# Who makes the low half of x's even blocks: VectorE from PSUM, or ScalarE and GpSimd through a copy

## The reference

```
mask = arange(L) < length[:, None]                 # one length per batch row
K    = 2 * Re(sum_n Cs[h,n] * exp(dtA[h,n] * l))   # one kernel of 1024 taps per head
y    = (causal convolution of x*mask with K + x*mask*D) * mask
logits = y @ route_w.T                             # 8 experts, the largest one is taken
wh   = one_hot(argmax) * max * (y @ A.T)           # 8 experts x rank 16 = 128 columns
out  = x + wh @ Bw
```

## Time and profile before

| what | value |
|---|---|
| median of 3 runs | 603.43 us (603.25 to 603.48) |
| profiled execution | 603.22 us |
| its span, first to last instruction | 601.4 us |
| mean granted TensorE clock | 0.996 of full speed |

### The profile page before, as it was taken

The page is one execution under the profiler, slowest core; times in us unless marked ns, Lnnn a source line. Parts: engine busy times, 40 slices in busy tenths (PEclk is TensorE's granted clock), DMA queues, the critical chain, the costliest instruction groups (busy, mean ns, idle before and its releaser), DMA issues.

```text
span 601.4 us, 13400 instructions
## 1 busy us (share of the span) xinstructions
PE 583.0 (97%) x3657; PEld 530.3 (88%) x3657; DVE 489.7 (81%) x1370; ACT 318.7 (53%) x1064; POOL 384.1 (64%) x519
## 2 busy tenths in 40 slices
PE   3899999999999999999999999999999999999996
PEld 2788999999999999999999899999999989999994
DVE  7978888888878888887887878788787887878875
ACT  4757566645554654654565464455546446445420
POOL 4687677576667657657666765866666685675430
PEclk9999999999999999999999999999999999999998
DMA  7133534533443443453454344345344434434521
GB/s 139 58 95 116 155 100 142 159 102 142 154 125 120 151 153 98 147 159 98 142 155 124 124 151 140 111 146 158 96 146 156 116 130 151 137 110 150 157 82 71
DMA packets 37583, 77.65 MB, mean 129 GB/s; under 512 B 12476, under 2 KB 20862, under 8 KB 37510
## 3 DMA queue, kind: packets, MB, share of 16 engines
q1 hardware_dynamic: 28358, 43.76, 28.8%
q10 hardware_dynamic: 9152, 33.03, 13.4%
HBM read 43.16 MB, written 33.62 MB: 128 GB/s over the span
## 4 chain that ended last, share of the span: by engine, by line
PE 90%; DVE 3%; POOL 2%; issue 1%; ACT 0%; ACTq 0%; POOLq 0%; DVEq 0%
PE psYo L1084 19%; PE psZ L1109 19%; PE psO L1084 15%; PE psYe L1084 12%; PE psS L1084 11%; PE psO L1134 4%; PE psXe L1098 4%; PE psXo L1098 4%; PE psZ L1168 1%; DVE psS L941 1%; POOL Xlo L505 0%; POOL Slo L512 0%; DVE Sf L945 0%; POOL Tlo L497 0%; POOL Glo L490 0%
## 5 line engine op out<-in xcount | busy, mean ns | idle before, releaser
L512 POOL TENSOR_TENSOR Slo<-Sf,Shi 128x384 fp32r<-128x384 f32 x64 | 65.4, 1022 | 165.3 <-ACT Shi L661 165.3
L941 DVE SCALAR_TENSOR_TENSOR psS<-Sf,tab,psS 64x128 f32<-64x128 f32 x256 | 91.9, 359 | 46.5 <-ACT Sf L656 39.6
L1109 PE MATMUL psZ<-Wt,Y 128*128 128x136 f32 x1024 | 129.2, 279 | 0.0
L1109 PEld LDWEIGHTS psZ<-Wt,Y 128*128 128x128 f32 x1024 | 123.3, 190 | 0.1
L656 ACT ACTIVATE Sf<-psS 128x128 f32<-128x128 f32 x64 | 17.8, 278 | 196.3 <-PE psS L1084 196.3
L980 DVE TENSOR_TENSOR ost<-psO,xt 128x512 f32<-128x512 f32 x128 | 87.8, 690 | 1.6 <-PE psO L1084 1.4
L505 POOL TENSOR_TENSOR Xlo<-xeven,Xhi 128x512 fp32r<-128x512 f32 x63 | 81.6, 1295 | 0.0
L473 POOL TENSOR_TENSOR both<-coarse,fine 128x512 f32<-128x512 f32 x64 | 68.3, 1067 | 1.3 <-ACT fine L601 1.2
L964 DVE TENSOR_TENSOR wlo<-psZ,whi 128x128 fp32r<-128x128 f32 x64 | 18.7, 292 | 40.4 <-ACT whi L666 40.4
L1084 PE MATMUL psO<-Bw_hi,whi 128*128 128x512 f32 x128 | 50.5, 395 | 0.7 <-ACT whi L666 0.7
L1084 PE MATMUL psO<-Bw_hi,wlo 128*128 128x512 f32 x128 | 50.8, 397 | 0.0
(11 more groups left out here) (200 smaller groups left out, 1526.7 us busy)
## 6 DMA issues: line engine op xcount, KB each, us to landing
xt<-in_x_dram SPq DMA_DIRECT2D x64, 512.0 KB, 4.9
out_dram<-ost ACTq DMA_DIRECT2D x63, 512.0 KB, 5.1
Traw<-kdram SPq DMA_DIRECT2D x64, 128.0 KB, 2.9
kdram<-krow SPq DMA_DIRECT2D x64, 1.0 KB
A_nat<-in_L_ffn_A_dram SPq DMA_DIRECT2D x1, 512.0 KB, 5.5
B_nat<-in_L_ffn_Bw_dram SPq DMA_DIRECT2D x8, 64.0 KB, 3.6
out_dram<-ost SPq DMA_DIRECT2D x2, 256.0 KB, 2.0
lens_i<-in_itok_B_dram SPq DMA_DIRECT2D x1, 64.0 KB, 4.9
```

The costliest lines, as they stand in the source:

```text
L512: pool.tensor_tensor(Slo[h.s2][:, :], Sf[h.s2][:, :], Shi[h.s2][:, :].bitcast(F32), ALU.subtract).then_inc(slo_done, 1)
L941: dve.scalar_tensor_tensor(psS[to, new], Sf[h.s2][fr, old], tab2[fr, BR, h.n:h.n + 1], psS[to, new], ALU.mult, ALU.add).then_inc(brought_d ...
L1109: last = pe.matmul(psZ[:, 0:NW], Y[:, j, c, :], Wt[:, 2 * c + j, :], start=(j == 0 and c == 0), stop=(j == 1 and c == NE - 1), skip_group_ ...
```

## The change

VectorE makes the low part of both halves of x, straight from PSUM, for every head. ScalarE's copy `x_even`, its buffer `xeven` and its semaphore, and GpSimd's subtraction `x_lo` are dropped. In VectorE's step the subtraction of the odd blocks moves from in front of the routing chain to behind `b_lo`, and the subtraction of the even blocks stands right before it there; both are then in front of `w_lo`. `turn_x` now waits for `xlo_even` of the head before instead of for the copy.

```diff
@@ buffers and semaphores
-        xeven = sb("xeven", [P, HALF])
-        xeven_done = sem("xeven_done")
@@ GpSimd
-            def x_lo(h):
-                need(pool, xeven_done, h.n)
-                need(pool, y_mm, (h.n - 1) * 2)
-                pool.tensor_tensor(Xlo[h.s2][:, 0, :], xeven[:, :], Xhi[h.s2][:, 0, :].bitcast(F32),
-                                   ALU.subtract).then_inc(xlo_even, 1)
...
-                if head(1).there:
-                    x_lo(head(1))
@@ ScalarE
-            def x_even(h):
-                need(act, xlo_even, h.n)
-                act.activation(xeven[:, :], psX[0][:, :], ACT.Copy).then_inc(xeven_done, 1)
...
                 if head(1).there:
-                    x_even(head(1))
                     t_hi(head(1))
@@ VectorE
             def x_lo_even(h):
                 need(dve, xhi_done, h.n * 2 + 1)
+                need(dve, y_mm, (h.n - 1) * 2)
                 dve.tensor_tensor(eo(Xlo[h.s2], 0), psX[0][:, :], eo(Xhi[h.s2], 0).bitcast(F32),
                                   ALU.subtract).then_inc(xlo_even, 1)
...
                     carry(head(0))
-                if head(1).there:
-                    x_lo(head(1))
                 if head(-1).there:
                     largest(head(-1))
...
                     turn_k(head(2))
                     b_lo(head(2))
+                if head(1).there:
+                    x_lo_even(head(1))
+                    x_lo(head(1))
                 if head(-1).there:
                     w_lo(head(-1))
@@ TensorE, turn_x
-                if is_head(h, 1) and j == 0:
-                    pe.wait_ge(xlo_even, 1)
-                else:
-                    need(pe, *((xlo_odd, h.n) if j else (xeven_done, h.n - 1)))
+                need(pe, xlo_odd if j else xlo_even, h.n)
```

More of the change, by code:

```diff
@@ L551, in _ @@
             t_lo(first[0])
-            x_lo(first[1])
             g_lo(first[1])
@@ L750, in _ @@
             s_hi(first[0])
-            x_even(first[1])
             g_hi(first[1])
@@ L1066, in _ @@
             clamp(parts[1])
+            x_lo_even(first[1])
+            x_lo(first[1])
             turn_k(first[2])
```

## The result

The changed kernel takes 619.25 us (median of 4 runs, 618.52 to 621.6) against 603.45 us for the kernel before (median of 4, 603.25 to 603.75): a ratio of 1.0269, 95% interval 1.0245 to 1.0293. The profiled execution's span is 617.9 us, 16.5 more than before. The forecast was 621.5 us for that execution, 621.7 for a median, within 612 to 631.

What follows compares the result with a forecast made beforehand. TensorE was taken to bound the steady loop. A 0.23 us wait plus 0.08 us weight load, 0.31 per step over 59 steps, added 18.3 us: 621.5 us profiled, 621.7 median, range 612 to 631.

Steps and rivals of the forecast that it cites:

- TensorE bounds the step, slack 0.15 us: Steady loop: TensorE waits for nobody, and `wlo` is ready 0.15 us before `up` would have to wait.
- Only 0.12 us of the moved subtraction come back: Before the routing chain: of the odd subtraction's 0.60 us, 0.12 return; the rest becomes VectorE's wait for `project`.
- E: The end of `project` in a step, from which later starts are counted in us.
- The rival by which the cover holds: Routing chain starts early enough that `wlo` is in time and nothing changes: 603.4 us, chance 0.08.
- The pair takes 1.20 us: Before `wlo`: the even and odd subtractions from PSUM together occupy VectorE for 1.20 us.
- The full-length rival: Each subtraction holds VectorE for its full 0.67 to 0.69 us, the pair 1.36: 631 us, chance 0.07.
- The stall: At `up`: TensorE stands still for late `wlo`, 0.23 us per step.
- The restart of 0.08: First two matmuls of `up` after the wait: an unhidden weight load adds 0.08 us per step.
- the lower bound of 0: The least cost allowed for the weight load after `up`'s wait, since a transpose might explain the 0.08 us: 616.8 us.
- 59 steps: The loss falls in steps 3 to 61; steps 1, 2 and those after 61 add nothing.
- Faster by the start-up: Step 1: less GpSimd work removes TensorE's 1.20 us wait for `Grev`, steady loop unchanged: 602.2 us, chance 0.05.
- The busy times: Whole kernel: VectorE gains some 43 us of busy time, ScalarE loses 37, GpSimd 82.

Runs made afterwards that it cites:

- both halves alone: Two kernels: the changed kernel with the odd subtraction back before the routing chain, 604.04 us; the kernel before with only that subtraction moved behind `b_lo`, 603.51 us.
- the third subtraction: The changed kernel with one more subtraction of 512 columns behind the pair, its result unread: 655.23 us.
- the kernel with the split wait: The changed kernel with `up` waiting for `wlo` before its third matmul instead of its first: 602.41 us, ratio 0.9982.

## Why the prediction was right

**TensorE bounds the step, slack 0.15 us.** Right. Until the pair is late nothing happens (both halves alone within about 0.1% of the kernel before), behind that each 0.60 us costs 0.60 us per step.

**Only 0.12 us of the moved subtraction come back.** Right: the chain starts at E + 0.03 (forecast E + 0.04), after a wait of 0.40 us for `project`. The rival by which the cover holds needed it 0.19 before E; it falls. One reading is off without effect: in the kernel before, `carry` ended at 260.09 (a row of 259.74 and 0.35), 0.35 before E and not 0.44.

**The pair takes 1.20 us.** Right: 269.07 to 270.26 is 1.19. The full-length rival falls with it, and the third subtraction settles it: over the 59 steps it adds 35.2 / 59 = 0.60 us per step with rows of 0.67. The Trainium skill (VectorE: DVE Perf Modes, The DRAIN you can't avoid) has the next instruction wait until the pipe is empty, but adds that one that is not held starts earlier. The rows here, 0.60 apart and 0.67 long, go with the addition, which the prediction left out.

**The stall.** Forecast 0.23, measured 3.27 - 3.08 = 0.19, since the chain to `Blo` took 1.36 (1.37), and `wlo` started 0.03 earlier and took 0.27 (0.29). The mechanism holds; the term is 0.04 too large.

**The restart of 0.08.** Right in size: 270.95 - 270.64 = 0.31, now without a transpose in front of it, so the lower bound of 0 falls. That it is the weight load which costs this is read from its place, 0.03 us before its matmul, and was not tested by itself. The Trainium skill (TensorE: Matmul & The Clock Gate, Step-by-step: what each phase is for) lets a weight load go ahead of running matmuls; here, behind a semaphore wait, it came at 270.61, 0.08 after `wlo` had ended, so this rule does not take the price away. In the kernel with the split wait, whose first matmul does not stand at `wlo`, the load came 0.17 before its matmul (262.96 and 263.13).

**59 steps.** Right: `up` starts at E + 3.27 to E + 3.32 in steps 3 to 61 and at E + 3.08 again in step 62. The counts of the waits say nearly the same: the 59 waits for `project` include step 1 and the last head, the 61 idle weight loads include steps 1 and 2. Step 1 costs nothing, as forecast; step 2 is 0.19 us longer (9.46 against 9.27), which the forecast had put at nothing.

**Faster by the start-up.** It falls: in the kernel with the split wait, whose GpSimd has the list of the changed kernel, TensorE still waits 1.18 us for `Grev` in step 1. In the changed kernel it is 0.77, mostly because `up` of that step is late itself. The 1.20 us could be had by GpSimd's order, in either kernel.

**The busy times.** The signs are right, two sizes are not: VectorE gained 29 us (forecast 43) and ScalarE lost 29 (37); GpSimd lost 79 (82). The forecast took each row whole, while busy time counts rows that lie over one another once. For ScalarE that is the whole difference: its rows fell by 37.7 us, and 9.0 of that had lain over others. VectorE's new rows are 42.4 us as forecast; 4 us more lie over others (`Blo`, the pair and `wlo` by 0.07 to 0.08 each time), and its other rows became about 9 us shorter, 5.2 of it in the sine tables' `frac` (32 rows, 384 ns in the mean before, 222 after). Why they did is not shown. No term of the sum rests on them. The wait of `up`'s weights appeared, but under "issue", not under `wlo`.

The sum: 16.1 us over the 59 steps, 0.19 + 0.08 = 0.27 each, instead of 59 x 0.31 = 18.3. The median lies 2.4 us under the forecast of 621.7, about what the stall's 0.04 makes in 59 steps.

## What to carry to other kernels

Work moved to an engine that is busy 81% is not priced by its share but by the gap in which it lands: find which wait ends last on both sides of the place, add the instruction's spacing, and compare with the slack, here 0.15 us. Two edits that are free alone can cost together, since each uses the same gap. Before work is moved back, look at the wait that it runs into: a wait placed in front of the first of three matmuls, of which only the third needs the operand, was the whole 2.7%.

A transfer's issue is an instruction in an in-order queue too: a store that waits for late adds held up the next step's first copy for 21 us in all.

## What was not expected of the hardware

TensorE's busy share stayed at 97% while it stood still in each step: 0.19 us of pause and 0.08 of restart lie almost wholly under modelled matmul ends. The idle time of the weight loads for `up` is what moved, 23.3 us against 4.6 before (groups of TensorE's weight loads, the row of the kernel before and that of the changed kernel):

```profile
L1084 PEld LDWEIGHTS psO<-Bw_hi,whi 128*128 128x128 f32 x128 | 24.0, 187 | 4.6 <-ACT whi L666 0.9
...
L1068 PEld LDWEIGHTS psO<-Bw_hi,whi 128*128 128x128 f32 x128 | 23.9, 187 | 23.3 <-issue 19.5 <-ACT whi L649 0.9
```
